# Experts' gate and up of two batches as seven block products, attention's end in a new order, weight block sums on GpSimd

## What is computed

```python
weights = _golden_weights(x, Wr, temperature)     # router: x @ Wr, sigmoid, zones, top 2
gate = jnp.einsum('btd,edf->betf', x, Wg)         # 8 experts, 512 x 512 each
up = jnp.einsum('btd,edf->betf', x, Wu)
h = jax.nn.silu(gate) * up
e_out = jnp.einsum('betf,efd->betd', h, Wd)
out = jnp.einsum('bte,betd->btd', weights, e_out)
```

## Time and profile before

| | |
|---|---|
| median of 3 runs | 2972.26 us (2971.87 to 2972.6) |
| span of the profiled execution | 2969.9 us |
| PE busy | 2949.0 us, 99% |
| DVE busy | 1819.7 us, 61% |
| ACT busy | 1230.8 us, 41% |
| POOL busy | 1143.3 us, 38% |
| experts' products | about 1891 us to 2961 us |

### The profile page before, as it was taken

The page is one execution under the profiler, slowest core; times in us unless marked ns, Lnnn a source line. Parts: engine busy times, 40 slices in busy tenths (PEclk is TensorE's granted clock), DMA queues, the critical chain, the costliest instruction groups (busy, mean ns, idle before and its releaser), DMA issues. The chain is left out here.

```text
span 2969.9 us, 38192 instructions
## 1 busy us (share of the span) xinstructions
PE 2949.0 (99%) x14014; PEld 2461.3 (83%) x14014; DVE 1819.7 (61%) x2571; ACT 1230.8 (41%) x2642; POOL 1143.3 (38%) x783
## 2 busy tenths in 40 slices
...
PEclk9999999999999999999999999999999999999999
...
DMA packets 62042, 135.39 MB, mean 46 GB/s; under 512 B 9248, under 2 KB 9632, under 8 KB 60832
## 3 DMA queue, kind: packets, MB, share of 16 engines
...
## 5 line engine op out<-in xcount | busy, mean ns | idle before, releaser
L771 POOL TENSOR_TENSOR ffn_in_lo<-ffn_inner,ffn_in_hi 128x512 fp32r<-128x512 f32 x191 | 249.5, 1306 | 1076.7 <-ACT ffn_in_hi L767 1076.7
L767 ACT ACTIVATE ffn_in_hi<-ffn_inner 128x512 fp32r<-128x512 f32 x192 | 121.4, 632 | 538.8 <-DVE ffn_inner L791 354.9
L44 PE MATMUL S<-xT_hi,ffn_w_hi 128*128 128x512 f32 x768 | 299.3, 390 | 0.0
L46 PE MATMUL S<-xT_hi,ffn_w_lo 128*128 128x512 f32 x768 | 298.8, 389 | 0.0
L45 PE MATMUL S<-xT_lo,ffn_w_hi 128*128 128x512 f32 x768 | 298.8, 389 | 0.0
L791 DVE TENSOR_TENSOR ffn_inner<-B,ffn_gated 128x512 f32<-128x512 f32 x64 | 44.3, 692 | 293.2 <-PE B L46 283.8
L791 DVE TENSOR_TENSOR ffn_inner<-S,ffn_gated 128x512 f32<-128x512 f32 x64 | 44.3, 692 | 291.4 <-PE S L46 284.9
L1951 POOL TENSOR_TENSOR lag_rnorm<-lag_norm,minus_half 128x8 f32<-128x8 f32 x64 | 105.4, 1647 | 298.9 <-DVE lag_norm L2215 298.9
L44 PE MATMUL B<-xT_hi,lag_w_hi 128*128 128x512 f32 x512 | 206.6, 403 | 0.5 <-DVE lag_c L1997 0.5
L46 PE MATMUL B<-xT_hi,lag_w_lo 128*128 128x512 f32 x512 | 200.8, 392 | 0.0
L44 PE MATMUL A<-xT_hi,lag_w_hi 128*128 128x512 f32 x512 | 200.6, 392 | 0.0
...
## 6 DMA issues: line engine op xcount, KB each, us to landing
...
lag_rot_q<-lag_r SPq DMA_DIRECT2D x128, 128.0 KB, 2.3
lag_rot_k<-lag_r SPq DMA_DIRECT2D x128, 128.0 KB, 2.3
...
```

What stands on the lines that cost most here:

```text
L44: pe.matmul(out, lh, rh, start=first and k == 0, stop=False)
L46: done = pe.matmul(out, ll, rh, start=False, stop=last and k == n - 1)
L767: act.activation(self.in_hi[t % 2][:, f, :], self.inner[f], ACT.Copy).then_inc(self.s_hhi, 1)
L771: pool.tensor_tensor(self.in_lo[t % 2][:, f, :], self.inner[f], f32(self.in_hi[t % 2][:, f, :]), ALU.subtract).then_inc(self.s_hlo, 1)
```

## The change

**Seven products for eight.** For a pair of batches and 128 inner features ("chunk" q), the 2 x 2 block product of (gate, up) weights by two halves of the contraction (256 each) with the two batches' rows is computed by Strassen's scheme in Winograd's form: 7 block products of K = 256 instead of 8. There are 32 chunks for batches 0 and 1, then 32 for batches 2 and 3. `Paired` does this, with `PairRows` for the blocks of rows. Block sums are needed of the weights (S1 to S4, for each chunk, on POOL: `sums`) and of the rows (T1, T2, T3, N4, once for each pair, on DVE: `PairRows.sum`). The results are formed in PSUM and SBUF: product 1 opens bank 0 and is copied out by ACT (`snap` 1), product 6 is added in the bank and copied (`snap` 2), then product 7 (`snap` 3), then product 4; DVE adds banks 1 and 2 to these copies (`corner`), multiplies (`inner`), and ACT and POOL split the inner product as before. Two chunks are in flight, in two sets of three banks.

**Other parts.** The weights of every chunk are split twice in the program, once for each pair. The router's product is one unsplit float32 matmul for each slice, 4 per batch, and its weights are computed for one pair at a time. Batches 2 and 3 are normalised, turned and routed during chunks 4 to 14 rather than ahead. Residual and norm of batch 0 start one step earlier, batch 1 gets its residual on DVE (`add_residual`), and the statistics of batch 0 stand behind other work on DVE. The order of PE, ACT, POOL, DVE and SP is rewritten from there to the end; the last unit has no order of its own any more.

```diff
+class Paired:
+    BLOCK = 2 * P
+    PARTS = {1: ("A11", "B11", 0), 2: ("A12", "B21", 1), 6: ("S2", "T2", 0), 7: ("S3", "T3", 0),
+             5: ("S1", "T1", 2), 4: ("A22", "N4", 0), 3: ("S4", "B22", 2)}
...
+    def sums(self, eng, q):
+
+        eng.wait_ge(self.s_raw[q % 2], (q // 2 + 1) * 32)
+        part = lambda block: self.part(q, block)
+        eng.tensor_tensor(part("S1"), part("A21"), part("A22"), ALU.add).then_inc(self.s_sum, 1)
+        eng.tensor_tensor(part("S3"), part("A11"), part("A21"), ALU.subtract).then_inc(self.s_sum, 1)
+        eng.wait_ge(self.s_sum, 4 * q + 1)
+        eng.tensor_tensor(part("S2"), part("S1"), part("A11"), ALU.subtract).then_inc(self.s_sum, 1)
+        eng.wait_ge(self.s_sum, 4 * q + 3)
+        eng.tensor_tensor(part("S4"), part("A12"), part("S2"), ALU.subtract).then_inc(self.s_sum, 1)
...
+        for k in range(2):
+            cols = slice(at + k * P, at + (k + 1) * P)
+            w_hi, w_lo = self.w_hi[q % 2][:, cols], self.w_lo[q % 2][:, cols]
+            pe.matmul(out, w_hi, hi[:, k, :], start=first and k == 0, stop=False, skip_group_check=not first)
+            pe.matmul(out, w_hi, lo[:, k, :], start=False, stop=False, skip_group_check=not first)
+            done = pe.matmul(out, w_lo, hi[:, k, :], start=False, stop=k == 1, skip_group_check=not first)
+        done.then_inc(self.s_p, 1)
...
+class Router:
...
+        for k in range(KC):
+            last = pe.matmul(bank[0:EXPERTS, :], self.w_f[:, k * EXPERTS:(k + 1) * EXPERTS], self.rows.rows[b][:, k, :],
+                             start=k == 0, stop=k == KC - 1)
...
@@ -1446,62 +1883,90 @@
-                turn2.turn(pe, 0, [A, S0, S1, B], norm_2.s_row)
+                rows.turn(pe, 0, [A, B, S0, S1], norm_2.s_row, lambda t: pe.wait_ge(s_sz, STEPS) if t else None, (0, 1))
                 pe.wait_ge(s_mix, STEPS)
                 turn_tiles(T, mixed, s_ot)
...
+                for q in range(2, last_chunk):
+                    experts.product(pe, 1, q + 1)
+                    downs(q, 1)
...
+                    experts.product(pe, 2, q + 1)
+                    downs(q, 2)
+                    experts.product(pe, 4, q)
+                    downs(q, 4)
...
+                    experts.product(pe, 3, q)
+                    downs(q, 3)
+                    turn_row(q, 0)
+                    experts.product(pe, 6, q + 1)
+                    downs(q, 6)
+                    experts.product(pe, 5, q + 1)
+                    downs(q, 5)
...
+                    experts.product(pe, 7, q + 1)
@@ -1758,74 +2217,125 @@
+                for q in range(2, last_chunk):
+                    if q + 2 <= last_chunk:
+                        experts.split_hi(act, q + 2, 0)
+                    experts.snap(act, 1, q + 1)
...
+                    experts.snap(act, 3, q + 1)
+                    if q in (2, turn_at + 1):
+                        experts.split_hi(act, q + 2, 1)
+                        experts.split_hi(act, q + 2, 2)
+                    if q == turn_at + 1:
+                        experts.again(act, "B22")
...
@@ -1932,56 +2442,80 @@
+                for q in range(2, last_chunk):
+                    if q + 2 <= last_chunk:
+                        experts.split_lo(pool, q + 2, 0)
+                    if q <= last_chunk - 2 and q not in BUSY:
+                        experts.sums(pool, q + 2)
+                        experts.split_lo(pool, q + 2, 1)
+                    experts.low(pool, 0, q)
...
+                    if q % 2 and q > 2 or q == last_chunk - 1:
+                        experts.down_split_lo(pool, q // 2)
...
@@ -2217,83 +2768,148 @@
-                accumulate(third, 2)
-                accumulate(third, 3)
-                statistics(0)
-                norm_2.aggregate(dve, 0)
+                gains(last_step)
+                statistics(0, (0,))
+                probabilities(last_step)
                 accumulate(before_last, 0)
                 accumulate(before_last, 1)
-                gains(last_step)
-                probabilities(last_step)
-                norm_2.normalise_on_vector(dve, 0, (2, 3))
-                turn2.low(dve, 0)
-                gated_output(last_step)
-                y_low(last_step)
+                statistics(0, (1, 2, 3))
+                norm_2.aggregate(dve, 0)
                 accumulate(before_last, 2)
                 accumulate(before_last, 3)
...
+                add_residual(1)
+                statistics(1)
```

1032 lines of the change are left out of this document (754 added, 278 removed).

## The result

The changed kernel takes **2926.47 us** (2926.17 to 2927.33, four runs) against 2972.14 us (2971.87 to 2972.6) for the kernel before in the same group of runs: ratio 0.9847, 95% interval 0.9833 to 0.9861. It is 45.7 us faster. The forecast was 2905 us with a range of 2890 to 2932, so the direction and the range held and the gain was 21.5 us smaller than forecast. Two thirds of the forecast gain came; where the rest went is the subject of what follows.

The account below looks back on a forecast made before the run. PE, busy 99% of the span, was taken as the bound. Terms -87.0 + 3.1 + 0 + 8 + 5.5 + 1.2 + 2 gave -67.2 us, from 2972.26 to 2905 us, range 2890 to 2932.

Parts of the forecast that it names:

- Matmuls removed, -87.0: Experts' products on PE: 3072 matmuls become 2688, 384 fewer at 0.2265 us each, -87.0 us.
- The sign that went with it: PE over the whole profile: busy time falls by 80 to 84 us, experts' matmuls stay 0.2265 us apart.
- Router, +3.1: Router's product: 48 split matmuls (10.9 us) give way to 16 unsplit float32 ones (13.9 us), +3.1 us.
- The steady chunk, 0: Chunks in steady running: no engine makes PE wait, 0 us, with up to 0.5 us per odd chunk in the range.
- The handover, +8: Loop's end to chunk 3: later first expert matmul and several PE waits, +8 us (0 to 15).
- The pair change, +5.5: First pair to second: T2's low part late, product 3 of chunk 32 waits for B22, +5.5 us (1 to 10).
- The close, +1.2: Kernel's end: batch 2's later normalisation delays the last batch's squares and last addition, +1.2 us (0 to 3).
- The clock, +2: PE behind the two expected holes: lower clock makes matmuls cost twice, +2 us (0 to 9).
- (b): Rival on odd chunks: ACT's queue is late past its 0.5 us spare, 31 us lost, 2936 us; chance 0.13.
- (c): Rival on the chunks: POOL becomes the bound, kernel slower than before, 3033 us; chance 0.05.
- (d): Rival on PE: 448 changes of product cost 0.1 us issue time each, 45 us, 2950 us; chance 0.06.
- (a): Rival on handover and pair change: they hide in other work, gain nearly whole, 2893 us; chance 0.18.

Follow-up runs that it names:

- e10: Changed kernel with product 5 computed twice in each of the 64 chunks, so eight block products as in the kernel before: 3003.5 us.
- e6: Changed kernel with three more ACT copies of 336 columns ahead of the down weights' high part in 26 odd chunks: 2947.94 us.
- e7: Changed kernel with two more POOL subtractions of 336 columns ahead of the second inner product's low part in 51 chunks: 2949.97 us.
- e1: Changed kernel with the second pair's route steps on DVE spread over chunks 17 to 27 instead of two blocks: 2915.84 us.
- e3: Changed kernel with POOL's sums and low parts in chunks 17 to 20 done on 8 columns only, route steps unmoved: 2916.12 us.
- e8: Changed kernel with e1's spread route steps, B22 and POOL's sums earlier at the pair change, and three reorderings at the handover: 2909.29 us.
- e11: e8 with POOL's chunk 33 sums further ahead, e9's divided normalisation and three first-route steps moved into chunk 2: 2904.87 us.
- e4: Changed kernel with batch 0's four statistics and aggregate on DVE ahead of the last probabilities and two accumulations, as before the change: 2928.21 us.
- e9: Changed kernel with tiles 2 and 3 of batch 0 normalised on DVE instead of ACT: 2929.12 us.

## Why the prediction was right, and where its sum was off

**Matmuls removed, -87.0.** Right, and e10 prices it by itself. In the plain chunks 1875 matmuls start in 425.00 us, 0.2267 us apart; in the trace of before it is the same from 2000 to 2900 us, and the earlier trace rows gave 0.2265. The sign that went with it did not come: PE's busy time was to fall by 80 to 84 us and fell by 69.5. Of the 38.7 us that eat of the gain (83.8 for matmuls and router, less 45.1) 24.4 are idle time; the other 14.3 lie inside the busy time, as matmuls at the lower clock and as steps that are longer than 0.2265 us but shorter than a record.

**Router, +3.1.** Right: the product of batch 0 takes from 1900.55 to the next start at 1904.08, 3.53 us, 0.88 per matmul against 0.87 taken.

```profile
1900.55 3.60 PE L1243 MATMUL O<-turned_rows,middle_router 128*8 128x512 f32 x8
1904.08 0.50 PE L1054 MATMUL S<-xT_hi,middle_w_hi 128*128 128x512 f32 x1
```

**The steady chunk, 0.** Right for a plain chunk, down to ACT's spare time of 0.5 us (0.43 in e6). POOL's at the down weights was less than it counted (1.7 us; 1.1 in e7). POOL's rows of after in 2500 to 2800, beside the earlier trace rows, confirm the two prices that no row of before had: 768 columns 1.85 us (taken 1.85), 256 columns 0.74 to 0.76 (taken 0.74).

```profile
L1102 POOL TENSOR_TENSOR middle_in_lo<-middle_slot,middle_in_hi 128x512 fp32r<-128x512 f32 x41 | 58.2, 1421 | 22.1 <-ACT middle_in_hi L1098 22.1
...
L1121 DVE TENSOR_TENSOR middle_slot<-middle_slot 128x512 f32<-128x512 f32 x21 | 25.7, 1222 | 1.9 <-ACT middle_slot L1092 1.9
...
L1009 POOL TENSOR_TENSOR middle_w_lo<-second_raw,middle_w_hi 128x768 fp32r<-128x768 f32 x10 | 18.5, 1849 | 1.4
...
L985 POOL TENSOR_TENSOR second_raw<-second_raw 128x256 f32<-128x256 f32 x10 | 7.4, 744 | 0.0
```

**This is also the term that was sized wrong.** The prediction wrote "I take **0**" for all chunks from one walk through a plain one. Chunks 4 to 19 are not plain: the change moved the normalisation, turning, router product and route of batches 2 and 3 into them, and none of these moved steps was costed there. They cost 7.2 us in chunks 3 to 16 (waits of 1.8, 0.7, 0.6 and some tenths, and steps a little too long around the transposes) and 7.7 us at the route, with 1.9 more at the lower clock behind its second wait. e1 and e3 show the route's part and its cause; for the 7.2 us only the wait at 1980.7, POOL's roots ahead of the down weights, was tried (in e8, where it is gone). The rest is open. So are the 1.6 us of the last chunks, half of them a wait of 0.8 us for a snap at 2894.92.

**The handover, +8.** 8.4 us without the clock, but behind the first expert matmul by another mechanism, so that 5.0 us for 4.8 is luck. The prediction named four waits there: for batch 1's rows, a corner, the router's second copy and the tables. PE's list has none of the first three, and behind the two table loads (1928.47 and 1930.71) ACT stands idle for 1.28 us before the snap that PE waits for. The two waits at 1935.70 (1.75 us) and 1944.99 (2.23) are for snaps. The first snap waited for POOL, whose inner product stood behind four sums; the second stood on ACT behind an inner product that DVE reached only at 1941.88, behind seven route steps of the first pair that took 7.0 us. In e8 and e11, where both orders are changed, 0.3 us of the first wait are left and nothing of the second. The first expert matmul's 3.4 us were read rightly, but neither link that the prediction put them down to could be taken back (e4, e9).

**The pair change, +5.5.** The wait, its place and its cause were forecast: B22's low part ends late, product 3 of chunk 32 waits 4.7 us (4.8 were counted), after a wait of 1.5 us for T2's low part (0.5 were counted). Added up, this is 5.3 us, which the prediction wrote as 5.5; the term is 6.5 us. T2's low part took 2.31 us on DVE, where 1.1 to 2 had been taken. POOL's down weights took 3.39 us beside DVE's operations, where 2.4 had been taken, and the sums and B22 stand behind them: the holding goes in both directions here, and the prediction had priced one.

**The close, +1.2.** The last addition begins 3.06 us behind PE's end (forecast 3.4, before 2.2), and the close costs 0.9. DVE waits here for ACT's square:

```profile
2917.22 0.15 DVE L602 TENSOR_SCALAR norm_std<-norm_std 128x1 f32<-128x1 f32 x1 [1.88 <-ACT middle_slot L595]
...
2917.76 0.74 DVE L1130 SCALAR_TENSOR_TENSOR x_tok<-B,expert_weight,x_tok 128x512 f32<-128x512 f32 x1
```

**The clock, +2.** Two holes were to cost 1.6 us each, 3.2, of which the sum took 2. It was three, 1.6, 1.9 and 1.6 us (at 1944.99, 2245.68 and 2433.96); the fall of the clock ahead of the first expert matmul cost nothing that can be seen. That no hole before was of such length is wrong for the whole trace: in before PE stands still for 3.4 us up to 274.28, and PEclk is 0.50 from there to 277.5. Behind the 5.3 us wait, PE's timeline and the window of one of these microseconds (PEclk is the third number from the end):

```profile
2245.68 0.76 PE L1054 MATMUL S<-xT_hi,middle_w_hi 128*128 128x512 f32 x1 [5.34 <-DVE middle_slot L1111]
2246.24 0.63 PE L1055 MATMUL S<-xT_hi,middle_w_hi 128*128 128x512 f32 x1
```

```profile
2247.00:2248.00 1.00, 1.00 (x4) 0.71 (x3) 0.39 (x1) 0.39 (x1) 0.53 (x1) 0.50 0.00 0
```

Behind the first of these, the steps are 0.43 us at 1.2 GHz and 0.2265 at 2.4. The Trainium skill (TensorE: Matmul & The Clock Gate, Why this matters for your kernels) warns of idle gaps between bursts of matmuls. The trace agrees, with 0.2 us lost for each of about eight matmuls, and shows it behind a hole of 2.2 us as well (at 1944.99, after one of 1.75).

**The rivals.** (b): snap 2 never made a plain chunk wait, but e6 shows it was 0.43 us away. (c) did not happen, since POOL was at 75% and its one overlap per chunk costs half a microsecond. (d): 448 changes of product cost nothing, since the plain windows have no idle time. (a), 2893 us, is not reached even by e11: the forecast's own 2905 is what the better orders come to, and that is chance: the forecast had 0 for the chunks and 2 for the clock, while e11 still loses about 10 us from the first expert matmul to chunk 16, 2.3 at the pair change and nothing to the clock there.
